# Mixture-of-experts stage: 15 tiles of 256 rows and 9 of 128 in turns, with the bf16 weight parts made beside each tile instead of in the layers

## What is computed

```python
def _L1_ffn_ref(X, Wg, bg, W1, W2, W3):       # X: 2048 tokens x 256
    logits = jnp.einsum('btd,de->bte', X, Wg) + bg
    topv, topi = jax.lax.top_k(logits, 2)
    w = jax.nn.softmax(topv, axis=-1)
    xs = X[:, :, None, :] * w[..., None]
    out = X
    for e in range(8):                         # W1[e], W3[e]: 256x1024, W2[e]: 1024x256
        h = silu(xs @ W1[e]) * (xs @ W3[e])
        y = h @ W2[e]
        out = out + where(topi == e, y, 0).sum(axis=2)
    return out
...
x = _layernorm(x + _L1_ffn_ref(x, ...))
```

## Time and profile before

| | us |
|---|---|
| median of 3 runs | 1763.68 |
| lowest, highest | 1758.65, 1769.99 |
| the profiled execution's own time | 1765.36 |
| its span, first to last instruction | 1763.5 |

### The profile page before, as it was taken

One profiled execution on the slowest core, in us unless ns is written; L12 is line 12 of the kernel. 1 busy time (PEld: TensorE's weight loads), 2 busy tenths in 40 slices (PEclk: granted clock), 3 DMA queues, 4 the chain that ended last, 5 costly groups with the idle time before them and its releaser, 6 DMA issues. The chain is left out here.

```text
span 1763.5 us, 46865 instructions
## 1 busy us (share of the span) xinstructions
PE 1435.4 (81%) x19776; PEld 1187.6 (67%) x19776; DVE 1056.8 (60%) x2444; ACT 647.7 (37%) x1410; POOL 409.5 (23%) x451
## 2 busy tenths in 40 slices
PE   5987985779898676997885699888572999999993
PEld 3885773559666445886763489667442888888882
DVE  5766677476756837576675666756843444344444
ACT  3223443433154343314534342244332444334431
POOL 0013141131313312112232311314112112221222
PEclk8798997879999887899997879999695999999997
DMA  7454021131021222110113112012004666766663
GB/s 264 180 194 158 26 72 37 58 101 41 28 63 32 60 73 67 46 51 26 38 38 107 61 62 63 2 38 84 13 13 165 242 209 224 251 223 211 236 197 107
DMA packets 87286, 183.46 MB, mean 104 GB/s; under 512 B 8642, under 2 KB 67266, under 8 KB 77250
## 3 DMA queue, kind: packets, MB, share of 16 engines
q1 hardware_dynamic: 75913, 165.20, 26.8%
q0 software_dynamic: 8160, 10.49, 3.0%
q10 hardware_dynamic: 3040, 5.25, 0.8%
HBM read 141.07 MB, written 58.21 MB: 113 GB/s over the span
## 5 line engine op out<-in xcount | busy, mean ns | idle before, releaser
L2201 PE MATMUL m_bank<-e_xT,e_w 128*128 128x256 bf16 x2208 | 245.6, 273 | 0.5 <-DVE e_xT L2270 0.5
L1950 POOL TENSOR_TENSOR e_room<-e_room 128x512 bf16<-128x512 f32 x96 | 112.9, 1181 | 547.3 <-ACT e_room L1944 547.2
L714 PE MATMUL bank<-arena 64*64 64x64 f32 (+2 forms) x6400 | 226.0, 230 | 12.9 <-DVE arena L904 3.7
L714 PEld LDWEIGHTS bank<-arena 64*64 64x64 f32 x6400 | 219.2, 141 | 23.4 <-issue 12.7
L2201 PEld LDWEIGHTS m_bank<-e_xT,e_w 128*128 128x128 bf16 x2208 | 216.3, 98 | 26.5 <-DVE e_xT L2270 0.9
L2283 DVE TENSOR_TENSOR e_h<-m_bank,e_silu 128x256 f32<-128x256 f32 x184 | 78.1, 424 | 202.1 <-ACT e_silu L2244 202.1
L2213 PE MATMUL m_bank<-m_xT,e_h 128*128 128x256 bf16 x1104 | 124.1, 273 | 0.0
L2213 PEld LDWEIGHTS m_bank<-m_xT,e_h 128*128 128x128 bf16 x1104 | 107.9, 98 | 12.3
L2244 ACT ACTIVATE e_silu<-m_bank 128x256 f32<-128x256 f32 x184 | 70.5, 383 | 124.3 <-PE m_bank L2201 124.3
L2122 POOL DMA_INDIRECT tokens<-e_y,e_ids x46 | 71.5, 1555 | 89.3 <-ACT e_y L2252 79.9
L977 ACT COPY arena<-bank 128x320 f32<-128x320 f32 (+1 forms) x96 | 37.5, 391 | 148.3 <-PE bank L714 147.9
(11 more groups left out here) (303 smaller groups left out, 2803.2 us busy)
## 6 DMA issues: line engine op xcount, KB each, us to landing
e_w<-parts SPq DMA_DIRECT2D x46, 1024.0 KB, 6.1
e_room<-E SPq DMA_DIRECT2D x96, 256.0 KB, 3.2
parts<-e_room SPq DMA_DIRECT2D x192, 128.0 KB, 2.9
m_xT<-parts SPq DMA_DIRECT2D x23, 1024.0 KB, 7.3
slots<-C_empty SPq DMA_DIRECT2D x5, 3536.0 KB
e_x<-slots SPq DMA_DIRECT2D x24, 272.0 KB, 6.2
w_rest<-W_rest SPq DMA_DIRECT2D x1, 3592.0 KB, 16.6
xz<-xT SPq DMA_DIRECT2D x8, 256.0 KB, 2.8
```

The lines of the kernel that those rows point to most:

```text
L714: last = pe.matmul(b[r, p * width:(p + 1) * width], lhs[r, 4 * g + p, :], rhs[r, 4 * g + p, :], start=True, stop=True)
L1950: pool.tensor_tensor(out=e_parts[:, j % 2, LOW], in0=e_whole[:, j % 2], in1=e_parts[:, j % 2, HIGH], op=ALU.subtract).then_inc(sem("e_low" ...
L2201: last = pe.matmul(bank[b][:, col:col + SLOTS], w[:, wp, c, f * P:(f + 1) * P], xeT[u][:, xp, c, :], start=j == 0, stop=j == len(terms) - 1)
```

## The change

- The experts get 24 tiles, fixed in size: 15 of 256 rows and 9 of 128. `SIZES` puts a small tile at each odd place up to 17, so tiles 0 to 17 alternate and 18 to 23 are of 256 rows. `dve_table` deals each expert its 256-row tiles first (as many as fit in 15) and the rest as 128-row tiles, with some ten small instructions more.
- The weight parts are no longer made in the layers. L1759, L1944, L1950 and L1766 are gone there, and the buffers for the parts in DRAM too. The weights lie in DRAM as float32, ordered so that a partition's share is contiguous.
- In the experts' stage each tile loads its own float32 weights in 6 pieces of 128x1024 (512 KB), q = 0, 1 (W1), 2, 3 (W3), 4, 5 (W2), each to one buffer `e_raw{q}`. ScalarE rounds a piece, VectorE subtracts (`split`). Where in `hidden(i)` that is done is written in `SPLIT_BESIDE`: group f: (0 for this tile or 1 for the next, q).
- The loops of the experts' stage are unrolled; the small tiles issue instructions of 128 columns in `hidden`, 2 transposes instead of 4, and 24 matmuls of 256 columns in `answer` instead of 48.
- The 5 transfers that clear `slots` become 13 smaller ones, each behind a named step of the first sequence.
- All tables in `ORDERS` are replaced, for the streams as well. The numbers of steps of programs 0, 1 and 4 are the same as before; those of program 2 fall away.

```diff
-TILES = (TOK * TOPK + E * (SLOTS - 1)) // SLOTS
+TILES = 24
+PAIR_TILES, SINGLE_TILES = 15, 9
+SIZES = [1 if i % 2 and i // 2 < SINGLE_TILES else ST for i in range(TILES)]
...
-                merged(sp, [stream(s, (sp_gated,), sp) for s in range(STREAMS)] + [sp_weights(sp), sp_clear(sp)], merge_order(ORDERS["sp"]))
+                merged(sp, [stream(s, (sp_gated,), sp) for s in range(STREAMS)] + [nothing(), sp_clear(sp)], merge_order(ORDERS["sp"]))
...
+        raw = [sb(f"e_raw{q}", [P, 1024]) for q in range(PIECES_OF_TILE)]
+        def piece(part, i, q):
+            if q < 4:
+                return w13[i % 2][:, part, q // 2, q % 2, :]
+            return w2[i % 2][:, part, 4 * (q - 4):4 * (q - 3), :].rearrange("p f d -> p (f d)")
+
+        SPLIT_BESIDE = {1: (1, 0), 2: (1, 1), 3: (0, 4), 4: (1, 2), 5: (1, 3), 6: (0, 5)}
...
+                def weights(i, which):
+                    e = sp.value_load(shared["expert"][0:1, COLUMN[i]:COLUMN[i] + 1], min_val=0, max_val=E - 1)
+                    for q in which:
+                        if i:
+                            sp.wait_ge(split_low[q], i)
+                        name, own = (("E1", "E1", "E3", "E3", "E2", "E2")[q], q % 2)
+                        sp.dma_start(raw[q][:], a[name][bass.ds(e, 1), :, own * 1024:(own + 1) * 1024].rearrange("o p n -> (o p) n"))\
+                            .then_inc(raw_in[q], 16)
+
+                weights(0, (0, 1, 2, 3))
+                rows(0)
+                rows(1)
+                weights(0, (4, 5))
+                weights(1, (0, 1, 2, 3))
+                for i in range(TILES):
+                    if i + 2 < TILES:
+                        rows(i + 2)
+                    if i + 1 < TILES:
+                        weights(i + 1, (4, 5))
+                    if i + 2 < TILES:
+                        weights(i + 2, (0, 1, 2, 3))
...
             def _(act):
+                def split(i, q):
+                    act.wait_ge(raw_in[q], 16 * (i + 1))
+                    act.copy(piece(HIGH, i, q), raw[q][:]).then_inc(split_high[q], 1)
...
+                        act.activation(silu[b][:, 0:wide], bank[b][:, 0:wide], ACT.Silu).then_inc(sd[b], 1)
                         if f:
-                            high(i, u, f - 1)
-                    high(i, u, FE - 1)
+                            high(i, f - 1)
+                        if f in SPLIT_BESIDE:
+                            ahead, q = SPLIT_BESIDE[f]
+                            if i + ahead < TILES:
+                                split(i + ahead, q)
+                    high(i, FE - 1)
...
             def _(dve):
+                def split(i, q):
+                    dve.wait_ge(split_high[q], i + 1)
+                    dve.tensor_tensor(piece(LOW, i, q), raw[q][:], piece(HIGH, i, q), ALU.subtract).then_inc(split_low[q], 1)
```

More of the change, by code:

```diff
@@ L160 @@
[L160 to L164, removed]
@@ L1914, in dve_table @@
+            c0, cf, part, cum, pairs, single, step, room, past, kept, start = (t[n] for n in (
+                "c0", "cf", "part", "cum", "pairs", "single", "step", "room", "past", "kept", "start"))
             ci = t["ci"].bitcast(I32)
-            for i in range(2):
-                dve.wait_ge(sem(f"e_parts_stored{i}"), 32 * (len(pieces) // 2))
-            jids = consts["jids"]
-            link(dve.scalar_tensor_tensor(c0[:], run[:], float(SLOTS - 1), consts["bases"], ALU.add, ALU.subtract))
+            jids, jrows, upto = consts["jids"], consts["jrows"], consts["upto"].rearrange("p (a b) -> p a b", a=E)
@@ new lines, in dve_table @@
+            link(dve.scalar_tensor_tensor(room[:, 1, :], single[:], -float(P), step[:], ALU.mult, ALU.add))
+            for k, cols in enumerate(own):
+                last = dve.tensor_tensor(past[:, cols], jids[:, cols, None].to_broadcast([P, cols.stop - cols.start, E]),
+                                         cum[:, k, None, :].to_broadcast([P, cols.stop - cols.start, E]), ALU.is_ge)
+            link(last)
+            for k, cols in enumerate(own):
+                dve.tensor_tensor(kept[:, cols], past[:, cols], room[:, k, None, :].to_broadcast([P, cols.stop - cols.start, E]), ALU.mult)
@@ L2215, in answer @@
                     last.then_inc(yf[u], 1)
[L2217 to L2227 removed]
+                turned(0)
+                turned(1)
+                hidden(0)
@@ L2284, in hidden @@
                             .then_inc(hr[b], 1)
                         if f:
[L2286 to L2296 removed]
+                            low(i, f - 1)
@@ new lines, in hidden @@
+                        if f in SPLIT_BESIDE:
+                            ahead, q = SPLIT_BESIDE[f]
+                            if i + ahead < TILES:
+                                split(i + ahead, q)
+                    low(i, FE - 1)
+                for q in range(4):
+                    split(0, q)
+                turned(0)
+                turned(1)
+                hidden(0)
+                for i in range(TILES):
+                    if i + 1 < TILES:
+                        hidden(i + 1)
+                    if i + 2 < TILES:
+                        turned(i + 2)
```

514 lines of the change are left out of this document (222 added, 292 removed).

## The result

| | before | after |
|---|---|---|
| median (us) | 1763.30 on the same chip | 1802.38, 4 runs, 1797.48 to 1803.03 |
| ratio, 95% interval | | 1.0213, 1.0175 to 1.0251 |
| profiled execution, span (us) | 1765.36, 1763.5 | 1797.48, 1795.1 |

The account below looks back on a forecast made before the run. TensorE bounds the experts before the change, no engine the layers; afterwards SyncE's queue order binds the experts. 1765.4 + 13 (experts) + 6 (clock) - 12 (layers) = 1772, median 1.7 lower: 1770 us, range 1735 to 1798.

Parts of the forecast that it names:

- Its 512 KB: Experts, piece 0's transfer: lands in 3.7 us, making 5.0 from buffer 5's release to landing, bounds 3.9 and 5.8.
- the ring: Experts: piece 0 queues behind piece 5, which awaits buffer 5's release; 15.1 us per small tile, 16.5 per large, 22 totalling 350.4.
- ScalarE's and VectorE's part: Experts, after piece 0 lands: rounding 1.04 us, subtraction 1.25, then five groups, 7.85 in small tiles or 9.25 in large.
- its 1799 us for the whole: Whole program by the skill's bandwidth page: landing 6.3 us after release instead of 5.0, 29 us more.
- the clock's 6: Experts, small tiles: TensorE's stops lower its clock, 0.7 us for each small tile, +6 us, bounds 0 and 17.
- the 12 of the prediction: Layers: gain from removing GpSimd's and ScalarE's weight steps, -12 us; bound below -49, table changes worth some 20.
- through with group 1 about 3.1 us after release: Experts: TensorE finishes the next tile's group 1 before piece 0 lands, so its part isn't on the chain.
- my first rival: Experts: pieces come in time and TensorE binds, -49 us there, 1703 us in all with the layers; chance 0.08.
- The third rival: Experts: TensorE's clock stays low about 10 us behind each small tile, 32 us instead of 6, 1796 us; chance 0.17.
- 30 either way: Layers, sign in the new profile: a change differing over 30 us from some 12 earlier means tables, not removed steps, decide.
- my estimate of 15 for GpSimd's work beside VectorE: Layers: weight steps cause half of some 30 us of VectorE's stretching, so 15; about half of it was let pass.
- At nothing: Clearings, `dve_table`'s steps and first tile's roundings priced at nothing; if uncovered, the table 2 us, the last piece's rounding 2.3.

Follow-up runs that it names:

- e13_only0: Changed kernel, with pieces 1 to 5 loaded for the first tile only, so later tiles move just piece 0 and rows; stage 388.4 us, no ratio.
- e2_deep: Changed kernel with two buffers for each of the six pieces, SyncE's list in the same order; ratio to before 0.9845, stage 379.8 us.
- e1_order: Changed kernel with SyncE's list issuing pieces in the order their buffers come free; ratio to before 0.9838, 1735.0 us, stage 380.1.
- e9_both_again: e5_both run once more on another chip; ratio to before 0.9652, stage 345.5 us.
- e5_both: e1_order's list, plus turning of tile i+2's rows moved from behind hidden(i+1) into its group 4; ratio to before 0.9655, 1720.0 us, stage 345.9.
- e4_held: Changed kernel with one more SyncE wait: piece 1 goes out only when piece 0 has landed; stage 475.3 us, no ratio.
- e7_tables: e5_both with the layers' old tables for TensorE, VectorE, ScalarE and GpSimd, without the weight steps; ratio to before 0.9731, 1736.5 us.
- e3_alone: Changed kernel, with pieces 1 to 4 loaded for the first tile only, so pieces 5, 0 and rows move; stage 423.6 us, no ratio.

## Why the prediction was wrong

**The step that failed** is the bullet "Its 512 KB: ... I take 3.7 ... Together 5.0 from release to landing, bounds 3.9 and 5.8". The mechanism was right: the wait stands in SyncE's list, the ring runs through piece 0, ScalarE's and VectorE's part is 10.0 and 11.3 us (my 10.1 and 11.5), and a cut of the list takes the time away. The term was mis-sized: 5.9 us of landing in place of 3.7, 7.2 from release to rounding in place of 5.0, times 22, is 48 us, and so the rings are 398.8 instead of 350.4. The bounds were too narrow as well: 4.5 was taken from a 1024 KB transfer at its quickest. The row beside it, 7.0 in the median "with another beside it", was the case of piece 0, which has piece 5 ahead and three pieces and the rows behind it; I took the rows "without a neighbour" for a transfer that is never without one. `e13_only0` gives piece 0 that solitude and has my stage within some 3 us. Part of that agreement is luck: at most in the small tiles, 9 of the 22 rings, was it the landing that held ScalarE; in the 13 large ones it was a path that I had left out, of nearly the same length (below, with the experts). The Trainium skill's page "DMA: Bandwidth & Descriptors", section "Bandwidth", which I set aside, came nearer with its 6.3 us from release to landing, where the trace has 7.2; its reason there, small transfers, isn't what the runs show, since the same 512 KB land in 3.6 to 3.9 us when alone. That its 1799 us for the whole is so near to the 1802 is luck, since other terms were off too.

**The sum.** The stage took 53 us more than I had, the clock's 6 came to about nothing, and the layers gave 22 more: 25 in all, which is what parts the profiled execution's 1797.5 from the sum of 1772. Had the layers gained only the 12 of the prediction, the miss would have been twice as large.

**Point by point, the experts.** Head, from the first matmul to the first release, 16.3 us (predicted 14.4), rings 398.8 (350.4), tail, behind the last release, 23.2 (20.5): 438.3 against 385.3. TensorE's part was said to be "through with group 1 about 3.1 us after release". This was wrong too, though hidden by the larger error: it left out that hidden(i+1) waits for the rows' low part, behind all of hidden(i) in VectorE's list. With no transfer in the way (`e2_deep`) the first rounding starts 5.2 us after the release when a small tile ends and 5.4 in the row of large ones at the end, where I gave 5.0 with the transfer. So even a landing of 2 us wouldn't have brought my first rival: the ring has a second path of nearly the same length, and `e1_order` ends on it. Behind a large tile that goes over to a small one it was 1.7 to 4.8.

**TensorE's clock.** The stage's mean is 0.92, against 0.99 in the earlier trace rows and 0.98 in `e9_both_again`. In the ring above a low stretch, at the 1.2 GHz level, began while TensorE stood still (it had stopped at 1448.06). The window before it, and its own:

```profile
1441.00:1450.20 9.20, 7.06 (x64) 5.89 (x61) 9.20 (x16) 7.93 (x15) 0.00 (x0) 1.00 0.57 161
1450.20:1457.00 6.80, 4.83 (x46) 4.83 (x47) 2.56 (x8) 1.69 (x6) 1.87 (x3) 0.50 0.61 161
```

The clock fell as forecast, but for longer: between 1340 and 1766 it was low 13 times, seven times for 6.8 us and six times for 3.4. In this ring the place was another than forecast too (TensorE idle from the answer's end to 1452.17, for `e_xT`, not in group 6), and the stretch was over before piece 0 landed at 1458.94. The +6 came to about nothing here: all 22 first roundings waited for a transfer, not for TensorE, and the time from first rounding to last subtraction, 10.0 or 11.3 us, varies by 0.6 at most. The third rival, the clock as the cause, has nothing for it: where the ring was cut the clock was back at 0.97 or 0.98 without anything done about it. The low clock was a consequence of the waits. Where TensorE's path is the last one, though, a low stretch costs what the prediction said. `e5_both` had two in its stage, of 3.4 us each, and behind each of them one ring of 16.1 us where its likes took 14.5: 1.65 us, against the 1.7 of the prediction.

**The layers.** -34.2 us where I took -12, inside the bounds of -49 and +20, and more than the "30 either way" that I had named as the sign that the tables decide; they gave about half of it. The 34.2 is itself good to about 10 us only: on one chip the same layers took 1320.7 us in `e1_order` and 1330.0 in `e4_held`. The experiments split it: `e7_tables`, at 0.9731, is 47 us under before, of which the stage is 26, so removing the steps gave the layers some 21; the new tables gave 16.5 more on their chip (I gave them 0, within 20). There my estimate of 15 for GpSimd's work beside VectorE was right in size (16.9 us of time, 20.5 of VectorE's busy time), and halving it because neither engine is full was probably wrong; the 16.9 is too uncertain to settle it. The router's last step, came at 339.9 us for the first sequence, where it had come at 354.9.

**At nothing** stood up: the clearings, the table and the first splits left no wait that moved the end. The first tile's float32 pieces were there before its rows, as before.

## What to carry to other kernels

When a transfer is put on a chain, price it with the neighbours that the same queue gives it: what is issued within a microsecond or two ahead and behind. Issue prefetches in the order in which their buffers come free, and only then count buffers. Here that order was worth 58 us, more than the 34 that the layers gained. When one wait is last by a few microseconds, look for the next path before pricing its removal; the two edits together gave 0.9652 of before, which is 1702 us by the first chip's median.

## What the hardware showed that I hadn't expected

- Transfers issued close together on one queue delay each other, the later ones the earlier too: 512 KB alone landed in 3.6 to 3.9 us, with another 1.1 us ahead in 4.7 (with the rows behind it as well, 5.3), with three more and the rows behind in 5.9 (up to 7.5), and the third behind it in 9.5.
- One GpSimd subtraction of 1024 columns (2.12 us) held a VectorE step of 0.28 us for 2.18, a stop for nearly the whole step, where the earlier trace rows had let me think of a share. A product that reads a PSUM bank took its usual 0.42 beside the last one.
- VectorE's subtraction of 1024 columns takes 1.22 us, the extrapolation's 1.25 being close; 72 matmuls of 128 columns took 4.19 us in `e3_alone`, 58 ns each, where the earlier trace rows had 62.
- With six splits in every tile of 256 rows TensorE waited 3.1 us in 375.
